# Flamingo-style gated block on one core: h of units 9 to 18 turned by DMA instead of TensorE

## What is computed

```
x = x + tanh(g_xattn) * experts(layernorm(x), token, ctx, ctx, ctx)
x = x + tanh(g_ffn)   * bitlinear_ffn(layernorm(x))
experts:  for each row the expert e = min(token // 6250, 3) alone counts:
          a = h @ ctx[e].T;  y = (silu(a) * a) @ ctx[e].T
ffn:      out = bit(silu(bit(x, gate_w) + gate_b) * (bit(x, val_w) + val_b), out_w) + out_b
bit(x, w): x rounded to 8 bits by its row's maximum, w to -1, 0 or 1 by gamma, the mean of |w|
```

## Time and profile before

| | us |
|---|---|
| median of 3 runs (317.64 to 318.01) | 317.69 |
| the profiled execution: its time | 316.65 |
| the profiled execution: its span | 314.9 |
| TensorE busy | 293.4 (93%) |
| VectorE busy | 262.5 (83%) |
| GpSimd busy | 236.7 (75%) |
| ScalarE busy | 214.4 (68%) |

### The profile page before, as it was taken

How to read it: one execution, slowest core, us unless ns; L and a number is a source line. 1 busy time by engine, 2 the same in 40 slices (tenths; PEclk the granted TensorE clock), 3 DMA queues, 4 the chain that set the end, 5 groups by cost and what they waited for, 6 DMA issues and landing times.

```text
span 314.9 us, 5289 instructions
## 1 busy us (share of the span) xinstructions
PE 293.4 (93%) x1424; PEld 142.5 (45%) x1439; DVE 262.5 (83%) x499; ACT 214.4 (68%) x268; POOL 236.7 (75%) x260
## 2 busy tenths in 40 slices
PE   0979999999999999999889899999999999999981
PEld 0435555555555555544334344444444444444430
DVE  5869888868789986789998999998899889988850
ACT  4857688678866456786987788766976687664510
POOL 4554873798888779945776999898888987797722
PEclk9999999999999999999999999999999999999998
DMA  7689899674425822824152754546443542344171
GB/s 265 212 321 335 297 373 325 236 227 180 136 67 170 254 84 84 299 57 89 49 100 50 119 86 123 127 118 146 87 101 83 117 83 71 90 108 100 33 167 67
DMA packets 52549, 47.51 MB, mean 151 GB/s; under 512 B 44783, under 2 KB 44783, under 8 KB 50224
## 3 DMA queue, kind: packets, MB, share of 16 engines
q1 hardware_dynamic: 47968, 33.86, 39.6%
q0 software_dynamic: 4560, 13.40, 12.5%
HBM read 28.35 MB, written 10.00 MB: 122 GB/s over the span
## 4 chain that ended last, share of the span: by engine, by line
PE 82%; DVE 6%; DMA 5%; issue 2%; POOL 2%; ACT 1%; POOLq 0%; DVEq 0%
PE banks L585 31%; PE banks L652 16%; PE banks L661 16%; PE banks L676 14%; PE banks L592 3%; PE banks L562 2%; DMA raw<-in_ctx 2%; DVE raw L1117 1%; POOL w_both L443 1%; DMA out<-xg,raw 1%; DVE raw L1112 1%; DMA xg<-in_x,gather_at 1%; DVE xg L1142 1%; PE banks L548 1%; DMA tok<-in_itok_BxS 1%
## 5 line engine op out<-in xcount | busy, mean ns | idle before, releaser
L585 PE MATMUL banks<-w_both,turned 128*128 x444 | 102.0, 379 | 0.5 <-ACT turned L779 0.3
L443 POOL TENSOR_TENSOR w_both<-raw 128x1024 f32<-128x1024 f32 (+1 forms) x32 | 75.0, 2342 | 9.2 <-DVE raw L1112 7.2
L585 PEld LDWEIGHTS banks<-w_both,turned 128*128 128x128 f16 x444 | 43.4, 98 | 45.5 <-issue 1.6
L854 ACT ACTIVATE w_both<-w_both,magic,raw 128x1024 f32 (+1 forms) x31 | 38.2, 1234 | 36.4 <-DVE raw L1131 36.4
L676 PE MATMUL banks<-tern,xg 128*128 128x512 bf16 x248 | 59.6, 379 | 3.0 <-DVE xg L1142 1.0
L661 PE MATMUL banks<-tern,raw 128*128 128x512 bf16 x255 | 60.3, 379 | 1.3 <-DVE raw L1104 1.3
L652 PE MATMUL banks<-tern,raw 128*128 128x512 bf16 x251 | 59.9, 379 | 0.7 <-DVE raw L1112 0.4
L1104 DVE SCALAR_TENSOR_TENSOR raw<-banks,raw 128x1024 f32<-128x1024 f32 x32 | 40.9, 1278 | 5.7 <-issue 4.9
L1112 DVE SCALAR_TENSOR_TENSOR raw<-banks,raw 128x1024 f32<-128x1024 f32 x32 | 40.9, 1279 | 4.3 <-PE banks L661 4.3
L1117 DVE TENSOR_REDUCE raw<-w_both 128x1 f32<-128x1024 f32 x32 | 38.8, 1212 | 2.7 <-POOL w_both L443 2.6
L676 PEld LDWEIGHTS banks<-tern,xg 128*128 (+1 forms) x256 | 24.8, 98 | 33.7 <-DMA xg<-raw 1.8
(11 more groups left out here) (121 smaller groups left out, 397.5 us busy)
## 6 DMA issues: line engine op xcount, KB each, us to landing
raw<-in_ctx SPq DMA_DIRECT2D x4, 1024.0 KB, 6.5
raw<-in_L_ffn_gate_w SPq DMA_DIRECT2D x4, 1024.0 KB, 7.4
raw<-in_L_ffn_val_w SPq DMA_DIRECT2D x4, 1024.0 KB
raw<-in_L_ffn_out_w SPq DMA_DIRECT2D x4, 1024.0 KB, 5.2
raw<-x_low SPq DMA_DIRECT2D x8, 257.5 KB, 4.4
raw<-x_high SPq DMA_DIRECT2D x8, 257.5 KB, 4.1
raw<-in_L_ffn_gate_b SPq DMA_DIRECT2D x1, 1024.0 KB, 5.4
raw<-in_L_ffn_val_b SPq DMA_DIRECT2D x1, 1024.0 KB, 8.1
```

The source lines that it names most:

```text
L443: nc.gpsimd.tensor_tensor(z[:, t % 2, 2 * D * c:2 * D * c + width], g_sb[:, c, 0:width], v_sb[:, c, 0:width], ALU.mult).then_inc(z_made, 1)
L585: last = nc.tensor.matmul(acc[:, :], a[:, k * P:(k + 1) * P], flat(w[:, bass.ds(e4 + k, 1), :]), start=(k == 0 and i == 0), stop=(k == KD ...
L854: nc.scalar.activation(zq[:, a:b], flat(z[:, bass.ds(t % 2, 1), a:b]), ACT.Identity, scale=flat(sc[:, bass.ds(t, 1), 12:13]), bias=magic[: ...
```

## The change

For units 9 to 18 (`H_DMA = range(9, 19)`):

- VectorE's norm writes h to PSUM (hT_ps) and no longer to SBUF. ScalarE makes the high half and VectorE the low half from there, both into h_sb, which is read as f16 (`h16`).
- SP turns both halves with one transfer, 8 blocks of 128x128 in two bytes, into `hT_dma`, two buffers in the part of `tern` that is signed last. TensorE's `turn_h` is left out; product a waits on `h_turned`.
- norm, h_hi and h_low of unit j+2 stand in slot j (before: halves of unit j+1). On VectorE norm and the next unit's statistics come ahead of `gu(j)`.
- ScalarE's high half waits for the transfer before, since h16 is one buffer.
- All 24 sums are ScalarE's, SUMMED and SIGNED are set anew, and TensorE's loop over slots 15 to 17 is written out.
- In SP's queue the turns of units 9 to 14 stand between the last weight load and the loads of x1's rows; those go in pairs, each pair ahead of one of the turns of units 15 to 18.

```diff
-    SUMMED = (0, 0, 2, 5, 8, 11, 13, 14, 15, 16, 18, 20, 21, 21, 21, 21, 21, 21, 21)
+    SUMMED = (0, 0, 2, 5, 8, 10, 13, 15, 16, 17, 18, 20, 22, 24, 24, 24, 24, 24, 24)
-    SIGNED = (0, 0, 0, 0, 0, 0, 0, 2, 4, 6, 8, 8, 9, 10, 12, 14, 16, 17, 18)
-    DVE_SUM = 11
-    ACT_SUMS = SUMMED[-1]
+    SIGNED = (0, 0, 0, 0, 0, 0, 0, 1, 3, 5, 7, 8, 9, 10, 12, 14, 16, 17, 18)
+    H_DMA = range(9, 19)
...
+        h16 = h_sb[:, :].bitcast(f16)
+        hT_dma = tern[:, 2 * G + 6:2 * G + 10, :].bitcast(f16).rearrange("p (b i) d -> p b i d", b=2)
...
+            def turn_h(j):
+                sp.wait_ge(hTlo_made, j + 1)
+                if j >= H_DMA[0] + 2:
+                    sp.wait_ge(a_done, j - 1)
+                sp.dma_start_transpose(hT_dma[:, j % 2, :, :].rearrange("p i (k m) -> p (i k) m", m=P), h16).then_inc(h_turned, 16)
...
+            for j in H_DMA[:-4]:
+                turn_h(j)
             sp.wait_ge(signed, x_frees)
             stored_units(EARLY)
             sp.wait_ge(low_scattered, 16 * len(BOTH))
-            for t in range(EARLY):
+            for t, j in zip(range(0, EARLY, 2), H_DMA[-4:]):
                 load_rows(t)
+                load_rows(t + 1)
+                turn_h(j)
...
-                pe.wait_ge(abs_summed, min(G // 2 * (m + 1), ACT_SUMS))
-                if m == 2:
-                    pe.wait_ge(abs_summed_dve, PAIRS - ACT_SUMS)
+                pe.wait_ge(abs_summed, G // 2 * (m + 1))
...
-                    pe.wait_ge(hThi_made, j + 1)
-                    product(a_of(j), *hT_of(j), e4, (hTlo_made, j + 1),
+                    low_made = (hTlo_made, j + 1)
+                    if isinstance(j, int) and j in H_DMA:
+                        low_made = (h_turned, 16 * (j - H_DMA[0] + 1))
+                        pe.wait_ge(*low_made)
+                    else:
+                        pe.wait_ge(hThi_made, j + 1)
+                    product(a_of(j), *hT_of(j), e4, low_made,
...
-                if after:
+                if after and not (isinstance(j, int) and j + 1 in H_DMA):
                     turn_h(j + 1)
...
             def h_hi(j):
-                act.wait_ge(hT_done, j + 1)
+                if j in H_DMA:
+                    act.wait_ge(h_made, j + 1)
+                    if j == H_DMA[0]:
+                        act.wait_ge(hT_done, j)
+                    else:
+                        act.wait_ge(h_turned, 16 * (j - H_DMA[0]))
+                    nc.scalar.activation(h16[:, 0:D], hT_ps[:, :], ACT.Copy, scale=H_SCALE).then_inc(hThi_made, 1)
+                    return
...
                 silu(j)
-                if 0 < j < UNITS - 1:
+                if 0 < j < UNITS - 1 and j + 1 not in H_DMA:
                     h_hi(j + 1)
+                if j + 2 in H_DMA:
+                    h_hi(j + 2)
...
-                v.tensor_scalar(h_sb[:, :], unit_rows(j), mean_var[:, n, 0:1], rstd[:, n:n + 1],
+                if j in H_DMA:
+                    dve.wait_ge(hTlo_made, j)
+                elif j == H_DMA[-1] + 1:
+                    dve.wait_ge(h_turned, 16 * len(H_DMA))
+                v.tensor_scalar(hT_ps[:, :] if j in H_DMA else h_sb[:, :], unit_rows(j), mean_var[:, n, 0:1], rstd[:, n:n + 1],
...
+                early_norm = j + 1 in H_DMA and j + 2 in H_DMA
+                if early_norm:
+                    norm(j + 2)
+                    if j + 3 < UNITS:
+                        unit_stats(j + 3)
                 gu(j)
...
-                if 0 < j < UNITS - 1:
+                if 0 < j < UNITS - 1 and j + 1 not in H_DMA:
                     h_low(j + 1)
+                if early_norm:
+                    h_low(j + 2)
...
-                if DVE_SUM <= j < DVE_SUM + PAIRS - ACT_SUMS:
-                    sum_abs(ACT_SUMS + j - DVE_SUM)
```

More of the change, by code:

```diff
@@ L175, in hT_of @@
         def hT_of(j):
+            if isinstance(j, int) and j in H_DMA:
+                return tuple(hT_dma[:, j % 2, i, :] for i in range(2))
             return hTs[isinstance(j, int) and j == 1]
@@ L204, in gated_block @@
             sem("unit_bn"), sem("unit_aggr"), sem("x1_bn"), sem("x1_stats"), sem("eps_added"), sem("tile_rstds"))
-        wlo_pool, w_scaled, w_copied, abs_summed_dve = sem("wlo_pool"), sem("w_scaled"), sem("w_copied"), sem("abs_summed_dve")
+        wlo_pool, w_scaled, w_copied = sem("wlo_pool"), sem("w_scaled"), sem("w_copied")
+        h_turned = sem("h_turned")
         h_made, hT_done, hThi_made, hTlo_made = sem("h_made"), sem("hT_done"), sem("hThi_made"), sem("hTlo_made")
@@ L638, in _ @@
             slot(0, before=False, after=False, between=turn_second)
-            for j in range(1, GAMMA_SLOT[2] + 1):
+            for j in range(1, UNITS - 1):
                 slot(j, gamma=GAMMA_SLOT.index(j) if j in GAMMA_SLOT else None)
-            with pe.Fori(GAMMA_SLOT[2] + 1, UNITS - 1) as j:
-                slot(j)
             slot(UNITS - 1, after=False)
@@ L769, in h_hi @@
             def h_hi(j):
-                act.wait_ge(hT_done, j + 1)
+                if j in H_DMA:
[6 more added lines that the diff above has]
+                    return
+                act.wait_ge(hT_done, j + 1 if j < H_DMA[0] else j + 1 - len(H_DMA))
                 nc.scalar.activation(hT_of(j)[0], hT_ps[:, :], ACT.Copy, scale=H_SCALE).then_inc(hThi_made, 1)
@@ L787, in sum_abs @@
                     act.wait_ge(high_ready, 1)
-                nc.scalar.activation(flat(tern[:, 2 * p:2 * p + 2, :]), flat(raw[:, 2 * p:2 * p + 2, :]), ACT.Abs,
+                to = 2 * p if p < G else 2 * G + 12
+                nc.scalar.activation(flat(tern[:, to:to + 2, :]), flat(raw[:, 2 * p:2 * p + 2, :]), ACT.Abs,
                                      accum_out=abs_sum[:, p:p + 1]).then_inc(abs_summed, 1)
@@ L1002, in h_low @@
                 dve.wait_ge(hThi_made, j + 1)
-                v.scalar_tensor_tensor(hT_of(j)[1], hT_ps[:, :], H_SCALE, hT_of(j)[0], ALU.mult, ALU.subtract).then_inc(hTlo_made, 1)
+                hi, lo = (h16[:, 0:D], h16[:, D:2 * D]) if j in H_DMA else hT_of(j)
+                v.scalar_tensor_tensor(lo, hT_ps[:, :], H_SCALE, hi, ALU.mult, ALU.subtract).then_inc(hTlo_made, 1)
             def gu(j):
@@ L1055, in high_places @@
                                        ALU.add, ALU.add).then_inc(high_ready, 1)
-            def sum_abs(p):
-                dve.wait_ge(raw_loaded[p // 2], 16)
-                v.tensor_reduce(abs_sum[:, p:p + 1], flat(raw[:, 2 * p:2 * p + 2, :]), AX.X, ALU.add,
-                                apply_absolute_value=True).then_inc(abs_summed_dve, 1)
             w_low(0)
@@ L1163, in _ @@
                     gamma(GAMMA_SLOT.index(j))
-                if j + 2 < UNITS:
+                if j + 2 < UNITS and not early_norm:
                     norm(j + 2)
@@ L1167, in _ @@
                     w_low(4)
-                if 2 <= j < UNITS - 3:
+                if 2 <= j < UNITS - 3 and not early_norm:
                     unit_stats(j + 3)
+                if j + 2 in H_DMA and not early_norm:
+                    h_low(j + 2)
                 if j == 5:
                     high_places()
-                if DVE_SUM <= j < DVE_SUM + PAIRS - ACT_SUMS:
-                    sum_abs(ACT_SUMS + j - DVE_SUM)
                 if j == UNITS - 1:
```

## The result

The changed kernel takes **322.86 us** (median of 5 runs, 321.69 to 325.33) against 317.69: ratio 1.015, 95% interval 1.0106 to 1.0194, slower. Forecast were 319.5 us and a range up to 321.3: the side was right, the size too small by 3.4 us, and the range didn't hold the time. The profiled execution took 325.33 us (span 323.6), the longest of its five.

The account below looks back on a forecast made before the run. The prediction took TensorE alone, busy 93% of the span, to bound the kernel. Its terms, -4.4 + 3.1 + 2.8 + 0.3 = +1.8 us, on the 317.69 us median gave 319.5 us, range 316.4 to 321.3.

Parts of the forecast that it names:

- The slot of 5.62 us: TensorE's stretch from one gated product's turn to the next: 6.05 us before, 5.62 without the turn of h.
- Ten turns, -4.4 us: TensorE's turns of h for units 9 to 18 go, 0.44 us each on the chain: -4.4 us.
- I cost the order at nothing: Making norm and h's halves two units ahead costs 0, with about 0.6 us of VectorE per slot as cover.
- The three sums: Three absolute sums move from VectorE to ScalarE, which has 3 us spare in slot 13: no effect.
- First place: Unit 9's turn stands behind the last out_w load in SP's queue: +3.1 us (2.2 to 4.0) in slot 9.
- It lands at 75.4 (74.6 to 76): Landing of unit 9's turn behind the out_w load, where product a wants it at 73.1: first stall 2.3 us.
- Second place: x1's rows 6 and 7 stand behind unit 17's turn; product y in slot 17 waits: +2.8 us (1.8 to 3.8).
- lands at +10.9 to +11.2: Landing of x1's row 7, in us after slot 15's start, taking 4.1 to 4.4 us from issue.
- +0.3 for tile 0's turn: Bias loads, with tile 0's turn behind them, come later, before the feed-forward stage: +0.3 us for TensorE (0 to 1.0).
- The rival of the round trip: Single h buffer's loop through the transfer sets the pace if transfers take over 4.3 us: 322.5 us, chance 0.14.
- a hidden wait: The wait for x1's row loads is hidden, so the second stall is absent: 316.7 us, faster, chance 0.12.
- a punctual first turn: Unit 9's turn is served beside the out_w load, so not late; second stall 2.8 to 3.6: 317.0 us, chance 0.12.

Follow-up runs that it names:

- e8: Changed kernel with unit 9's turn issued ahead of the last out_w load and GpSimd's first x1 statistics split in two parts; 315.66 us, ratio 0.9928.
- e12: Changed kernel with five turns by DMA (units 14 to 18) instead of ten, and GpSimd's statistics split in two parts; 316.95 us, ratio 0.9959.
- e9: e8 with a second h buffer and a semaphore for each buffer; 316.71 us, ratio 0.9929 against the kernel before.
- e6: Kernel before the change with only all 24 absolute sums put on ScalarE, no turn by DMA; 318.20 us, ratio 1.0007.
- e10: Changed kernel with two buffers for h before it is turned, nothing else; 320.68 us, ratio 1.0062.
- e7: Changed kernel with GpSimd's rstd of tiles 0 to 3 in slot 15 and tiles 4 to 7 in slot 17, no transfer moved; 318.96 us, ratio 1.0033.
- e2: Changed kernel with x1's rows loaded in fours, so all eight are ahead of unit 17's turn; 318.78 us, ratio 1.0006.
- e13: Changed kernel measured once more, on one chip with e14; 324.94 us, ratio 1.0182 against the kernel before.
- e14: e1 measured once more, on one chip with e13; 321.83 us, ratio 1.0103 against the kernel before.
- e1: Changed kernel with unit 9's turn issued ahead of the last out_w load, x1's rows still in pairs; 323.63 us, ratio 1.0151.
- e5: Changed kernel with nine turns by DMA, unit 9's staying on TensorE; 322.69 us, ratio 1.0143.
- e4: Changed kernel with 17 idle matmuls in slot 9 ahead of product a, to keep TensorE's clock up; 322.76 us, ratio 1.0149.

## Why the prediction was right and wrong, by its steps

**The slot of 5.62 us: right.** Slots 11 to 13 and 16 of the changed kernel take 5.61 or 5.62. But slots 14 and 15 take 6.36 and 5.94, over the 5.8 us that the prediction set as a sign of being wrong, and the feed-forward stage starts at 142.75 and not at about 136.

**"Ten turns, -4.4 us": the turns are right, the order at nothing is the step that failed.** The turns are gone from TensorE, but with both places mended (e8) the gain is 2.3 us. Over slots 8 to 17 the kernel before takes 60.9 us in its profile, e8 58.2: 2.7. The other 1.7 us is what "I cost the order at nothing", with 0.6 us of VectorE as cover, left out. Half of it, 0.87 us, is in slots 8 and 9: the prediction priced a normal slot and not the passage from the old order to the new one, where VectorE is late (the lines under e12). The rest is in slots 12 and 14 to 16, of 5.79 to 5.95 us each. In slots 13 to 15 ScalarE waits 1.10 to 1.48 us for the turn of the unit before, and VectorE's low half waits for ScalarE:

```profile
107.78 0.60 ACT L797 ACTIVATE h_sb<-banks 128x512 f16<-128x512 f32 x1 [1.30 <-DMA tern<-h_sb]
```

So the turns' landings use up the cover there; that e9, with two buffers, has short slots 14 to 16 fits, though its time shows no gain.

**The three sums: right**, nothing (e6).

**First place: place and mechanism right, the size right by the times and wrong in the profile.** Product a of unit 9 was to begin at 75.4 after a stall of 2.3, 3.1 in all (bounds 2.2 and 4.0; by the terms shown they come to 2.3 and 3.7). In the profile it began at 78.52 after 3.80, with slot 9 itself starting 0.96 us later than drawn, and slot 9 was 6.55 us longer than before. Two steps failed there. "It lands at 75.4 (74.6 to 76)" took the gather of unit 11 and the load's end as in the profile of before. The gather took 3.57 to 3.85 us in e10, e7 and e2, where TensorE waited 1.57, 1.91 and 1.94 us, but 5.59 in the changed kernel's profile and 5.91 in e13's, where it waited 3.80 and 7.15; why it was longer isn't known. And nothing in the sum stood for the clock, which costs 2.5 us of product a and 0.5 of y (3.21 against 2.75) in this row. In e2 and e7 slot 9 is 3.0 and 3.8 us over 5.62, within the bounds. By the ratios the place is worth 3.3 us between e7 and e8 and 2.5 between e13 and e14, but nothing between e1 and the changed kernel. That 3.1 is close to the first two is in part luck, since the clock, which fell in e7's profile, had no term.

**Second place: right in this profile, too small in the others.** Rows 6 and 7 landed at S(17), forecast S(17)-0.4 to -0.1; ScalarE's turned half was ready at S(17)+6.1, forecast +5.8; the slot was 3.2 us over 5.62, forecast 2.8. But in e1, e5, e13 and e14 the wait was 4.35 to 4.83 and the clock fell behind it. The step that failed is "lands at +10.9 to +11.2", with 4.1 to 4.4 us for row 7 from the earlier trace rows: from the issue of row 6 to GpSimd's start it was 4.4 us in this profile (forecast as 4.7 to 5.0) and 5.6 to 6.0 in those four, and again nothing stood for the clock. By the ratios the place is worth 3.7 us with the first stall there (changed against e7), and 5.6 to 7.1 without (e14 and e1 against e8).

**"+0.3 for tile 0's turn": right in size**, 0.53 us of wait at the start of the feed-forward stage in the changed kernel (142.75), 1.01 in e7 and none to speak of in e8.

**The sum then**, by the ratios: the change without its two places (e8) gives -2.3 us where the forecast had -4.1 (-4.4 and 0.3), and the two places together take 7.1 where it had 5.9. Both errors point the same way, and they make the 3 us by which the forecast was short: 1.8 is the order that was costed at nothing, 1.2 the two places, of which the second is the one that was priced too low.

**The rival of the round trip** (322.5) named the nearest time. It said that transfers over 4.3 us decide, and there were such (4.47, 5.95). It holds in part, in the small waits of e8's slots 12 to 16. It isn't what bounds the kernel: with one buffer e8 is as fast as e9 with two. The rivals of a hidden wait and of a punctual first turn fell, both waits being there.

**The page that spoke against the change** (the Trainium skill, VectorE: DVE Perf Modes, "The three transpose paths") agrees with the side of the result and not with its size: eight blocks landed in 3.1 us at best, where its 1309 ns for each block, taken one after another, would be 10.5, an estimate from that page. Its "Rules for kernel authors" send a 128x128 transpose to TensorE where PSUM will do. What lost the time here is what shares the queue with the turns, and what waits behind them, and with that mended the change is a gain (e8), against that rule.

**What stays open.** In the first job moving the first turn gained nothing (e1, and e5 in the next one, against the changed kernel's first ratio), in the last one 2.5 us. The intervals of the changed kernel (1.0150 and 1.0182) and of e1 (1.0151 and 1.0103) overlap, so both may be one effect of 1 to 3 us seen through scattered stalls; that the second stall grows when the first goes is not excluded. Why rows 6 and 7 land in 4.4 us at one time and 6.0 at another wasn't found. What the clock's falls cost in the median isn't shown: taken away in one place (e4), the time stayed.

## What to carry to other kernels

A transfer put into a queue is only as early as what stands ahead of it: look up, for each step moved there, what is issued before it and what now stands behind it, and then who waits in line on the engine that needs it. Here two such places turned 2.3 us of gain into 4.8 of loss, and a cure for the larger one was not to move the transfer but to make its consumer ask for less (e7: four tiles' statistics instead of eight). The slot in which an old order passes into a new one is priced by itself and not as a normal slot (here 0.85 us). And a stall on TensorE is priced with a range of landings and not the one that the profile happened to show, and with the matmuls behind it at half clock, 1.4 to 2.5 us for 12 of them in these profiles.

## What the runs showed of the hardware

**The clock fell after idle times that don't order by length.** TensorE's granted clock fell to 0.50 behind waits of 1.91 us (e7), 2.77 (e10, slot 17), 3.60 (e4) and 3.80 (changed), and stayed at 1.00 behind 1.57 (e10, slot 9), 1.94 (e2) and 3.04 (changed, slot 17). In this last one TensorE was idle from 130.37 to 133.41 without a fall:

```profile
76.46 2.76 PE L601 MATMUL banks<-w_both,tern 128*128 x12 [1.94 <-DMA tern<-h_sb]
```

```profile
131.00:132.00 1.00, 0.00 (x0) 0.00 (x0) 0.40 (x1) 1.00 (x2) 1.00 (x2) 1.00 0.00 0
132.00:133.00 1.00, 0.00 (x0) 0.00 (x0) 0.00 (x0) 1.00 (x2) 0.82 (x2) 1.00 0.00 0
133.00:134.00 1.00, 0.59 (x3) 0.38 (x4) 0.70 (x3) 0.75 (x2) 0.99 (x3) 1.00 0.64 106
```

The first line is e2's, the three windows are the changed kernel's. Where the clock fell, the 12 matmuls behind the wait took 4.11 us (e4), 4.45 (e7, e10, e14) or 5.30 (changed, e1, e5, e13) instead of 2.75. So a stall of 2 to 3 us may or may not cost another 1.7 (e7 and e10 against e2 and slot 17 of the changed kernel). That this is part of why e1's six runs scatter from 320.6 to 325.2 is likely and not shown, since only one of them has a profile.

**A transposing transfer's landing varies threefold.** The same 8 blocks landed in 3.1 us at the least. Unit 9's turn took 3.2 us ahead of the 1 MB load (e8) and 6.2 to 9.5 us behind it in the same queue (changed, e2, e4, e7, e10, e13). A load ahead isn't the only way to be late: unit 11's turn took 7.45 us in e9 with no weight load ahead of it, beside scatters that took 7.3 us.
